# Self-attention of a fused decoder layer: the softmax divisor applied when the probabilities are split, in place of a divisor spread by TensorE and multiplied into the output

## The reference, cut to what matters

```python
x = x + _L0_attn_ref(_layernorm(x, axis=-1), L0_attn_w_qkv, L0_attn_w_out)
# within it, for 16 heads of 32:
q = q / scale
scores = jnp.einsum('bqhd,bkhd->bhqk', q, k)
scores = jnp.where(causal_mask[None, None], scores, NEG)
attn = jax.nn.softmax(scores, axis=-1)
out = jnp.einsum('bhqk,bkhd->bqhd', attn, v).reshape(b, s, HIDDEN)
return out @ w_out
```

## Time and profile before

| | |
|---|---|
| time, median of 3 | 730.67 us |
| the profiled execution's own time | 727.35 us |
| its span, first to last instruction | 725.6 us |
| busy share of the span: PE, DVE, POOL, ACT | 91%, 76%, 44%, 42% |
| self-attention | about the first 343 us of the span |
| mean granted TensorE clock | 0.978 of full speed |

### The profile page before, as it was taken

One profiled execution on the slowest core, in us unless ns is written; L12 is line 12 of the kernel. 1 busy time (PEld: TensorE's weight loads), 2 busy tenths in 40 slices (PEclk: granted clock), 3 DMA queues, 4 the chain that ended last, 5 costly groups with the idle time before them and its releaser, 6 DMA issues.

```text
span 725.6 us, 18923 instructions
## 1 busy us (share of the span) xinstructions
PE 662.2 (91%) x5896; PEld 585.6 (81%) x5897; DVE 549.2 (76%) x1657; ACT 307.9 (42%) x991; POOL 318.7 (44%) x545
## 2 busy tenths in 40 slices
PE   4758999999999989898999999999999998788994
PEld 4648888888888878786989898989898987566883
DVE  4767878787878788883578787878797967786663
ACT  2445666566666676661313232323232425322220
POOL 3368666665757677771400101010101242347652
PEclk9978999999999999999999999999999999889997
DMA  7395976666566655871970516151614484656520
GB/s 260 115 188 100 155 123 140 125 136 138 129 142 121 144 105 120 172 149 48 337 260 3 147 27 158 15 150 24 160 14 146 106 219 112 233 174 203 173 91 1
DMA packets 143070, 97.26 MB, mean 134 GB/s; under 512 B 110766, under 2 KB 114990, under 8 KB 142640
## 3 DMA queue, kind: packets, MB, share of 16 engines
q1 hardware_dynamic: 137360, 84.10, 48.7%
q0 software_dynamic: 5664, 12.61, 5.4%
HBM read 58.24 MB, written 18.77 MB: 106 GB/s over the span
## 4 chain that ended last, share of the span: by engine, by line
PE 37%; DMA 4%; DVE 4%; issue 3%; POOL 2%; ACT 1%; SPq 0%; DVEq 0%; ACTq 0%; POOLq 0%
PE b_bank L65 34%; DMA slots<-r_entry,r_slot_i 1%; DMA k_tab<-slots 1%; DVE w_lo L1578 1%; DMA bias_sb<-in_wo 1%; PE b_bank L1896 1%; PE b_bank L1480 1%; DVE w_lo L1117 1%; POOL w_lo L1363 1%; DMA stage<-x2n,k_gather_no 1%; DVE b_smax L1594 1%; PE b_bank L1531 0%; ACT w_hi L1407 0%; ACT w_hi L1417 0%; ACT b_prob L1424 0%
## 5 line engine op out<-in xcount | busy, mean ns | idle before, releaser
L513 ACT ACTIVATE prob<-prob,shift 128x128 f32<-128x128 f32 (+1 forms) x256 | 114.6, 449 | 116.1 <-POOL shift L424 115.6
L65 PE MATMUL b_bank<-w_hi 128*128 128x256 f32 (+1 forms) x528 | 106.7, 324 | 4.4 <-DVE w_lo L1578 4.2
L65 PE MATMUL a_job<-w_hi 128*128 128x256 f32 (+1 forms) x488 | 94.8, 318 | 14.9 <-DVE w_lo L716 7.1
L1407 ACT CAST w_hi<-b_bank 128x256 fp32r<-128x256 f32 (+1 forms) x128 | 52.8, 450 | 128.4 <-PE b_bank L65 117.3
L65 PE MATMUL b_bank<-w_lo,w_hi 128*128 128x256 f32 (+1 forms) x528 | 103.7, 319 | 0.0
L65 PE MATMUL b_bank<-w_hi,w_lo 128*128 128x256 f32 (+1 forms) x528 | 103.7, 319 | 0.0
L737 DVE CUSTOM_DVE_ANT_0 prob<-a_s,mask 128x128 f32<-128x128 f32 (+1 forms) x256 | 79.8, 348 | 30.0 <-PE a_s L613 29.9
L65 PEld LDWEIGHTS a_job<-w_hi 128*128 128x128 f32 x488 | 71.5, 196 | 24.7 <-DVE w_lo L716 7.8
L65 PEld LDWEIGHTS b_bank<-w_hi 128*128 128x128 f32 x528 | 80.5, 190 | 12.3 <-DVE w_lo L1578 5.6
L745 DVE TENSOR_TENSOR p_part<-prob,p_part 128x384 f16<-128x384 f32 x128 | 78.5, 613 | 14.0 <-POOL p_part L431 12.4
L65 PE MATMUL a_job<-w_lo,w_hi 128*128 128x256 f32 (+1 forms) x488 | 87.9, 303 | 0.0
(11 more groups left out here) (201 smaller groups left out, 1116.6 us busy)
## 6 DMA issues: line engine op xcount, KB each, us to landing
stage<-in_w SPq DMA_DIRECT2D x5, 1024.0 KB, 10.4
xin<-in_x SPq DMA_DIRECT2D x8, 512.0 KB, 4.2
xr<-in_x SPq DMA_DIRECT2D x8, 512.0 KB, 4.0
x<-xr SPq DMA_DIRECT2D x8, 512.0 KB, 3.2
xin<-x SPq DMA_DIRECT2D x8, 512.0 KB, 10.2
stage<-in_ctx_t SPq DMA_DIRECT2D x8, 512.0 KB, 3.6
stage<-in_ctx SPq DMA_DIRECT2D x8, 512.0 KB, 5.2
xr<-x SPq DMA_DIRECT2D x8, 512.0 KB, 6.3
```

The costliest lines, as they stand in the source:

```text
L65: ins = pe_matmul(out, a, b, start=first and i == 0, stop=last and i == len(steps) - 1)
L513: a = nc.scalar.activation(prob[:, e % NPROB, cols], prob[:, e % NPROB, cols], ACT.Exp, scale=-1.0, bias=shift[:, e, q:q + 1], accum_out=r ...
L1407: nc.scalar.copy(hi, src).then_inc(job_hi, 1)
```

## The change

The probabilities are normalised before the product with the values, and not the output after it. Every edit is in the self-attention:

- ScalarE takes the maximum from DVE directly (`nmax`), with no instruction of POOL between. After the exponentials of a head it writes the sum times 2^-15 (`usum`, 128 x 2).
- POOL raises that to the power -1 (`rinv`, a tensor_tensor of 128 x 2), waits for it, and writes the high part of `prob` times `rinv` in two tensor_scalar instructions (128 x 128 and 128 x 256) with a scalar for each partition.
- DVE's low part is `prob` times `rinv` minus the high part, in two scalar_tensor_tensor instructions.
- The reciprocal on DVE, the spread copy and `ot_lo` on POOL, the two matmuls of a group with the identity (each is two records, so four rows of the trace), the copy on ScalarE and the multiply on DVE go. The high and low parts of the output are taken from PSUM, one slot earlier than before, the low one by DVE.
- The residual add of y is a scalar_tensor_tensor with the factor 2^-15.

```diff
-        HI_LAG, LO_LAG, DMA_LAG, RINV_LAG, WIDE_LAG, AV_LAG, R_LAG, ON_LAG, OT_HI_LAG, OT_LAG = 1, 2, 2, 2, 3, 7, 7, 8, 9, 10
+        HI_LAG, LO_LAG, DMA_LAG, AV_LAG, OT_HI_LAG, OT_LAG = 1, 2, 2, 7, 8, 9
...
# POOL, in a slot
-                e = head_at(h, 0, n)
-                if e is not None:
-                    pool.wait_ge(mx_done, n * H + h + 1)
-                    pool.sem_inc(tick_pool, 1)
-                    nc.gpsimd.tensor_scalar(shift[:, e, :], nmax[:, e, :], LN_UNIT, None, ALU.add).then_inc(shift_done, 1)
                 t = head_at(h, HI_LAG, n)
                 if t is not None:
-                    pool.wait_ge(ex_done, n * H + h - HI_LAG + 1)
+                    pool.wait_ge(sum_done, n * H + h - HI_LAG + 1)
                     pool.sem_inc(tick_pool, 1)
+                    nc.gpsimd.tensor_tensor(rinv[:, t, :], usum[:, t, :], less[:], ALU.pow)\
+                        .then_inc(rinv_done, 1)
                     wait(pool, pt_in[t % HG], groups_before(h, HI_LAG, n) * 16)
                     pool.sem_inc(tick_pool, 1)
-                    nc.gpsimd.tensor_copy(p_part[:, t % NPROB, 0, :], prob[:, t % NPROB, :]).then_inc(p_hi_done, 1)
...
+                    pool.wait_ge(rinv_done, n * H + h - HI_LAG + 1)
                     pool.sem_inc(tick_pool, 1)
...
+                    for q, cols in ((0, slice(0, P)), (1, slice(P, 3 * P))):
+                        a = nc.gpsimd.tensor_scalar(p_part[:, t % NPROB, 0, cols], prob[:, t % NPROB, cols],
+                                                    rinv[:, t, q:q + 1], None, ALU.mult)
+                    a.then_inc(p_hi_done, 1)
...
# ScalarE
-                    act.wait_ge(shift_done, n * H + h + 1)
+                    act.wait_ge(mx_done, n * H + h + 1)
...
+                    act.wait_ge(ex_done, n * H + h + 1)
+                    nc.scalar.activation(usum[:, e, :], rsum[:, e, :], ACT.Copy, scale=UNIT).then_inc(sum_done, 1)
...
-                    nc.scalar.copy(o_sb[g % 2][:], o_ps[:, 1, :]).then_inc(rs_done, 1)
+                    nc.scalar.copy(ot_hi[:, g, :], o_ps[:, :]).then_inc(ot_hi_done, 1)
...
# PE, after the product with the values
                 m.then_inc(av_done, 1)
-                pe.wait_ge(wide_done, before + 1)
-                for q in range(TB):
-                    m = nc.tensor.matmul(o_ps[:, 1, q * P:(q + 1) * P],
-                                         rinv_wide[g % 2][:, q, :, :].rearrange("p j d -> p (j d)"), ident[:],
-                                         start=True, stop=True)
-                m.then_inc(r_done, 1)
...
# DVE
-                    nc.vector.tensor_tensor(p_part[:, t % NPROB, 1, :], prob[:, t % NPROB, :], p_part[:, t % NPROB, 0, :],
-                                            ALU.subtract).then_inc(p_done, 1)
+                    for q, cols in ((0, slice(0, P)), (1, slice(P, 3 * P))):
+                        m = nc.vector.scalar_tensor_tensor(
+                            p_part[:, t % NPROB, 1, cols], prob[:, t % NPROB, cols], rinv[:, t, q:q + 1],
+                            p_part[:, t % NPROB, 0, cols], ALU.mult, ALU.subtract)
+                    m.then_inc(p_done, 1)
...
-                    nc.vector.tensor_tensor(o_sb[g % 2][:], o_ps[:, 0, :], o_sb[g % 2][:], ALU.mult).then_inc(on_done, 1)
...
-                    nc.vector.reciprocal(rinv[:, g, :, :], rsum[:, g, :, :]).then_inc(rinv_done, 1)
...
+                    nc.vector.tensor_tensor(ot_lo[:, g, :], o_ps[:, :], ot_hi[:, g, :].bitcast(F32), ALU.subtract)\
+                        .then_inc(ot_done, 1)
```

More of the change, by code:

```diff
@@ L91, in self_attention @@
     scale = float(HD) ** -0.5
[L92 removed]
+    UNIT = 2.0 ** -15
     NPROB, NPT = HG, 2 * HG
@@ L111, in self_attention @@
         mask = sb("mask", [P, 2 * P])
-        nmax, shift = sb("nmax", [P, H, TB]), sb("shift", [P, H, TB])
+        nmax = sb("nmax", [P, H, TB])
         prob = sb("prob", [P, NPROB, 3 * P])
@@ L115, in self_attention @@
         pt = sb("pt", [P, NPT, 2 * 3, P], F16)
-        rsum, rinv = sb("rsum", [P, G, TB, HG]), sb("rinv", [P, G, TB, HG])
-        rinv_wide = [sb(f"rinv_wide{i}", [P, TB, HG, HD]) for i in range(2)]
-        o_sb = [sb(f"a_o_sb{i}", [P, S]) for i in range(2)]
+        rsum, usum, rinv = (sb(f"{n}", [P, H, TB]) for n in ("rsum", "usum", "rinv"))
+        less = sb("less", [P, TB])
         ot_hi, ot_lo = experts.place(7, S, D)
@@ L469, in _ @@
                     slot(n, h)
-        CONSTS = 5
+        CONSTS = 6
         @block.scalar
@@ L536, in slot @@
                     nc.scalar.copy(hi, src).then_inc(ctx_hi, 1)
-                g = group_at(h, R_LAG, n)
+                g = group_at(h, OT_HI_LAG, n)
                 if g is not None:
-                    before = groups_before(h, R_LAG, n)
-                    wait(act, ot_done, before - 1)
-                    act.wait_ge(r_done, before + 1)
-                    nc.scalar.copy(o_sb[g % 2][:], o_ps[:, 1, :]).then_inc(rs_done, 1)
+                    if g == 0 and not (isinstance(n, int) and n < 1):
+                        act.wait_ge(job_done, job_at("y1", n) + 1)
+                    act.wait_ge(av_done, groups_before(h, OT_HI_LAG, n) + 1)
+                    nc.scalar.copy(ot_hi[:, g, :], o_ps[:, :]).then_inc(ot_hi_done, 1)
             for h in range(H):
@@ L624, in values @@
                     pe.wait_ge(v_mid_done, v_at(first_use, of) + 1)
-                wait(pe, on_done, before)
+                wait(pe, ot_done, before)
                 for j in range(HG):
@@ L708, in evac @@
                     rows = xr[:, int(j[1]), :]
-                    nc.vector.tensor_tensor(rows, bank(j)[:, :], rows, ALU.add).then_inc(job_ev, 1)
+                    nc.vector.scalar_tensor_tensor(rows, bank(j)[:, :], UNIT, rows, ALU.mult, ALU.add).then_inc(job_ev, 1)
                     return
```

44 lines of the change are left out of this document (9 added, 35 removed).

## The result

The changed kernel takes 815.66 us (median of four runs, 813.56 to 817.1) against 730.47 us (four runs, 729.9 to 733.01): ratio 1.1148, 95% interval 1.1124 to 1.1173. It is 85 us slower; the forecast was 735.7 with a range of 721 to 752. The span of the profiled execution grew from 725.6 to 811.5 us.

The account below looks back on a forecast made before the run. PE was taken to bound steady sequences (34.80 of 35.75 us), POOL sequence 0. Sequence 0 +6.0, sequences 1 to 5 -5 x 0.45, sequence 6 +2.5, sequence 7 0, end -1.5: +4.8, rounded to +5, giving 735.7 us (range 721 to 752).

Parts of the forecast that it names:

- The price of the scalings: POOL, each head: the two scalings cost 0.9 us, between 0.7 (as casts) and 1.25 (as two-input instructions).
- The power's own result: POOL, each head: waiting for the power's result adds about 0.08 us, within a head of 1.70 us.
- The formula for POOL: POOL, steady sequence: 16 x 1.70 = 27.2 us, 33.0 with value parts and a power, plus 1.6 for collisions.
- the 5.8: POOL, steady sequence: four pairs of value parts at about 1.25 us and one power, beside the sixteen heads.
- the 1.6 of collisions: POOL, steady sequence: DVE and POOL hinder each other, taken as 0.1 us a head, 1.6 in all.
- POOL sets the whole stage: Rival, chance 0.17: scalings cost 1.15 us, a head 1.95, total +30 us; named 750; decides from about 1.75 a head.
- The other two have room and follow PE: 16.82: Two of a steady sequence's four group loops follow PE: 18.42 - 0.92 - 0.68 = 16.82 us.
- PE's part: PE: divisor's product gone, 0.46 us a group; y job's 0.68 us wait for ScalarE gone; 33.2 us a sequence.
- DVE's part: DVE: the low part in two pieces costs 0.66 us a head, where one cost 0.47; +3.0 us a sequence.
- the prediction's 0.19 and 0.1: DVE, each head: 0.19 us more for the split low part, and 0.1 us for contention with POOL.
- The first loop: Steady sequence, first of two tight loops through DVE: 8.91 - 0.41 + 0.47 = 8.97 us; the second 8.33.
- The shift: POOL loses the shift, pitch 0.28 us a head; ScalarE no longer waits for POOL, counted as nothing.

Follow-up runs that it names:

- a1: Changed kernel with POOL's two scalings replaced by plain casts (high part left undivided): 746.05 us, 1.0264 of the kernel before.
- c1: a1 with both parts of the output taken one slot earlier, as in c6: 728.03 us, 0.9938 of the kernel before.
- c6: Changed kernel with both parts of the output one slot earlier (ScalarE lag 7, DVE lag 8): 818.51 us, 1.1184 of the kernel before.
- b4: Kernel before without the spread product (output not divided), high part of the output one slot earlier: 724.43 us, 0.9879 of the kernel before.
- b1: Kernel before without PE's product that spreads the divisor (output not divided): 728.23 us, 1.0003 of the kernel before.
- b2: Kernel before, complete, without POOL's shift in front of the exponentials: 716.97 us, 0.9785 of the kernel before.
- a2: Changed kernel with POOL's scalings by constant 1.0, not a scalar for each partition (high part undivided): 790.47 us, 1.085 of the kernel before.
- c3: Changed kernel, reciprocal on DVE, output parts a slot earlier, ScalarE scaling 128 columns and POOL 256, no 2^-15 factor: 726.4 us, 0.9909 of the kernel before.

## Why the prediction was wrong, point by point

- **The price of the scalings** is the step that failed, and the change's loss follows from it. The pair was taken at 0.9 us and bounded by 1.25; it costs 1.47. "They have one tensor input, so they are nearer to the cast" was the wrong choice of row: even the upper bound was too low, as a scaling of 256 columns takes 930 ns and the two-input row that bounded it 752. Before, no POOL row multiplied a wide tensor by a scalar, and the bounds should have been open upwards. The 0.29 us fixed in that bound had no row either; the two measured forms give 0.40.
- **The power's own result** was taken at 0.08 us of waiting and costs 0.20. Together a head costs 2.40 us and not 1.70.
- **The formula for POOL held.** Put 2.40 in its place: 16 x 2.40 + 5.8 + 1.6 = 45.8 us for a steady sequence, against 44.66 measured. Of its two small terms the 5.8 measured 5.1, and for the 1.6 of collisions the heads took 1.1 more than 16 times 2.40. Sequence 0 would grow by 9 x 1.67 - 2.6 = 12.4 (13.5 measured), sequence 6 by 45.8 + 4.6 - 37.4 = 13.0 (12.8, 50.91 for 38.15 from scores to scores; the prediction's window of 37.40 ended 0.75 us before the next scores). The rival "POOL sets the whole stage" was the right mechanism, and its point of decision, 1.75 a head, was passed by far; its 1.95 was too small.
- **The loop with the y jobs** is the second failed step. "The other two have room and follow PE: 16.82" looked at PE's jobs and not at who frees `a_o`. The order of DVE's instructions had shown its part in the output moved a slot later, and in the prediction nothing was put against that. With casts it cost 3.2 us in that loop and 3.7 in a sequence (a1 against c1), and the move turned a1's 2.6% of loss into 0.6% of gain. In the change itself it lies behind POOL (c6).
- **PE's part.** The rows on `rinv_wide` are gone and the wait of the last y0 fell from 1.41 to 0.5 us. The product's worth was taken at up to 0.46 us a group: shown by b4 for three of the four loops. That nothing else would be late then was wrong (b1).
- **DVE's part was right in size, in part by luck.** The pitch of the two low parts is 207.71 - 207.05 = 0.66 us in this timeline of DVE, and that is also the median:

```profile
207.05 0.75 DVE L720 SCALAR_TENSOR_TENSOR p_part<-prob,rinv,p_part 128x128 f16<-128x128 f32 x2 [0.45 <-POOL p_part L429]
207.71 0.42 DVE L690 TENSOR_TENSOR w_lo<-a_job,w_hi 128x256 fp32r<-128x256 f32 x1
```

  The mean over a steady sequence is 0.81, where one low part had 0.54 (over the eleven heads with no wait behind it): 0.27 more, and the prediction's 0.19 and 0.1 make 0.29. But the 0.1 was meant for every head, and the surplus falls on the heads whose low part meets POOL's value parts (last section). The first loop was forecast at 8.97 us and took 8.99 in a1; the second at 8.33 and took 7.95, so DVE did not hold it. With the scalings cheap and the bank free in time (c1), the period is 33.84, and the loops alone had been forecast to sum to 34.1.
- **The shift.** Its removal was booked as 0.28 us of POOL's time and nothing for ScalarE. b2 shows it to be the one part of the change with a large gain, 15 us, because it stood on the way to the exponentials. In the change POOL sets the period, so the gain can't show; that is an argument, as no run of the changed kernel keeps the shift.
- **The rest of the program** took 386.1 us where it took 381.9, and in every faster version too it is 4 to 9 us longer than before (388.6 in b2, 391.3 in b4). In b2 PE waits 6.9 us there for DVE's `c_xt_lo`, for 2.7 before. But the profiled execution of the kernel before, at 727.35 us, is faster than each of its four timed ones, and those of b2 and b4 are the slowest of theirs. How much of the difference is the spread between executions stays open.

## What to carry to other kernels

Where a new operation has no row, bound it from above by more than the nearest row, or time it alone first: a scaling is arithmetic and not a cast, and on POOL that was a factor of two. Look for an engine's total first (16 heads times the new price against the period), then for who frees each buffer whose reader has moved. And take the small parts of a change one by one: here an instruction of 0.3 us between two engines was worth 2%, while the change around it cost 11%, and the repaired versions of the change gained no more than this part alone.

## What was not expected of the hardware

- POOL's tensor_scalar on one f32 input and f16 output costs 663 ns for 128 columns and 930 for 256, more than its subtraction of two 256-column inputs (752). That is not contention with DVE (a2). The Trainium skill, GPSIMD Engine Reference, section 4.1, puts one-input operations at roughly line rate; the casts bear that out (0.7 ns a column in a1), and the scalings, at 2.1 to 2.2 ns a column, do not.
- A scalar for each partition costs only 0.07 to 0.08 us more than a constant (a2).
- A scaling that waits for the power before it on POOL starts 0.21 us after the power's end, in 124 of 128 cases.
- Two waits of PE, 0.46 us before 155.26 and 1.29 before 157.56, were followed by a granted clock of 0.51 and 0.64 in the next two windows of 2 us (b1). The same two waits, 0.45 and 1.32 us, were followed by full speed one sequence later, and so was a wait of 0.68 alone. These waits alone do not decide it; what does was not isolated.
- DVE's pair of low parts takes 0.75 us at 207.05, though POOL's power runs from 206.98 for 0.72 beside it, and 1.26 at 203.85, beside POOL's subtraction of the value parts:

```profile
203.85 1.26 DVE L720 SCALAR_TENSOR_TENSOR p_part<-prob,rinv,p_part 128x128 f16<-128x128 f32 x2
```

```profile
203.89 0.68 POOL L399 TENSOR_TENSOR v_part<-v_rest,v_part 128x256 bf16<-128x256 f32 x1
```

  It is so throughout the changed kernel. Of the low parts of 256 columns, 75 ran beside a power alone and took 471 to 481 ns; the 27 in which POOL started its value subtraction took 480 to 495 ns more. POOL's subtraction did not pay: 678 ns in the mean, 752 before. In c3 it is POOL's scaling that pays, about 0.3 us, and DVE's low part in most cases does not. The Trainium skill, SBUF — State Buffer, "Who interferes with whom", says that a DVE instruction with two SBUF inputs contends with a GpSimd instruction that reads SBUF, and calls the shared ports an exclusive lock. The trace agrees for the value subtraction, and shows no cost beside a power of 128 x 2.
